# A layer norm folded into the dense layer behind attention, with smaller matmul bursts and a later weight preparation

## Chip, core and metric

The kernel runs on one core of a Trainium2 chip. The metric is the device time of one execution in microseconds (us), lower is better. TensorE is called PE here, ScalarE ACT, VectorE DVE, GpSimd POOL, and SyncE SP; SP issues all DMAs.

## What is computed

A pre-norm transformer block on x of 2 x 2048 x 1024 floats: latent attention with 32 heads whose keys have 4 numbers, and a dense layer with eight low-rank (LoRA) updates.

```python
x = x + attn(layernorm(x), ...)            # 32 heads, softmax over 2048 keys
# dense layer on layernorm(x):
h = jnp.einsum('bsd,nrd->nbsr', x, lora_A)
coef = (SCALE * lora_weights)[:, None, None]
lora_out = jnp.einsum('nbsr,nor->bso', h, lora_B * coef)
base = jnp.einsum('bsd,od->bso', x, W) + bias
# _layernorm: (x - mean) / sqrt(var + 1e-5), no gain, no bias
```

## The kernel before

The 4096 rows are taken in 8 chunks of 512 rows; a chunk is 4 tiles (t = 0 to 3) of 128 rows. A first stage (up to about 130 us) normalises x, computes the latents and stores query parts in DRAM. Then comes attention, chunk by chunk, in 128 steps each: step = 16 g + kt, g one of 8 groups of 4 heads, kt one of 16 key tiles. A step is: PE computes scores for 4 heads (L772), ACT takes two exponentials of 128 x 1024 (L562) out of PSUM, PE multiplies the results with the values (L783). PE's order is written out by hand in `attention`. In even steps PE does the scores and then the values of the two steps before; in odd steps it does the scores and then one piece of other work. Scores of a step wait for the first exponential of the step before (L770), values for their exponentials. PE is in order: a piece of work that waits holds scores and values behind it.

In chunk 0 the pieces are the preparation of weights (`prepare`): values (L701), LoRA (L707), the folded output weight (L719), biases (L726), and the dense weight `w_eff` in 16 blocks k: `turn_w(k)` transposes W (L737), `lora_update(k)` two steps later adds the LoRA product (L742), and DVE's `move_w(k)` (L1183 to L1189) takes both out of PSUM and splits the sum in a high and a low part. W lies in the stages `w_stage = [y, xn]`; SP's first load of a tile of x into y waits until the first half of W was read (L396), and the query loads `load_q` are queued behind it on SP. `W_BEFORE` blocks are prepared ahead of step 67, where the attention output of four groups is turned, the others after it.

In chunks 1 to 7 the pieces are the projection and the dense layer of the chunk before (`dense_beside`), all through the one PSUM bank SHARED. For each tile t: `project` (3 products into each of two halves, steps 7 and 9 for t = 0); DVE adds it to y and measures mean and variance (`residual`, `deviations`, 14 small operations in a chain); `normalise` writes xn (L995); from step TILE_AT[t] on PE turns xn in two pieces (`turn_xn`, L813) and DVE splits it into two parts (`move_xn`, L1017, L1019); then PE runs the dense layer in two halves of 24 products each (3 products for each of 8 blocks, L828), in bursts of at most `BURST` = 5 products: 5, 5, 5, 5, 4, one burst in each odd step; DVE adds the result to y (`add_dense`, L1239). POOL adds the attention bias to y when x has come, and the dense bias after xn was written (L470). Each tile has 28 steps: 4 for turning, 5 bursts, 2 projections of the next tile, 5 bursts.

After chunk 7's attention a tail does the same for the last chunk with nothing beside it: `project_last`, `turn_last` and `dense` on PE, on several banks.

Of the kernel before, what the change touches and what calls it, by code (L numbers as in the profile page):

```python
# [21 lines left out]
F32 = mybir.dt.float32  # L22
# [11 lines left out]
def build_block(nc, x, wq_d, bq_d, w_qk, b_qk, wkv_d, bkv_d, wv_u, bv_u, wo, bo,  # L34
# [38 lines left out]
    with ExitStack() as ctx:  # L73
# [76 lines left out]
        tight_f = sb("tight_f", [1, 1], F32)  # L150
        tight = sb("tight", [1, 1], I32)
        row_max = sb("row_max", [P, TT, H], F32)

        x_tiles = [y, xt_b]
        xn_tiles = [xn, xn_b]
# [24 lines left out]
        v_set, v_ln, v_lat, v_shift, v_rec, v_hi = (sem(n) for n in ("v_set", "v_ln", "v_lat", "v_shift", "v_rec", "v_hi"))  # L180
        prep_ps = sem("prep_ps")
        prep_ok = sem("prep_ok")
        x_in = [[sem(f"x_in{half}_{t}") for t in range(TT)] for half in range(2)]
        norm_ready = sem("norm_ready")
        xn_ready = sem("xn_ready")
# [86 lines left out]
        STORE_AT = [min(-(-(at + TILE_STEPS) // KT), G4 - 1) for at in TILE_AT]  # L272
# [162 lines left out]
        def _(pool):  # L435
# [137 lines left out]
        def _(pe):  # L573
# [155 lines left out]
            def turn_w(k):  # L729

                kb, half = k % KB, k // KB
                free_bank(PREP_W + 2 * k)
                pe.wait_ge(stage_in[half], 32)
                if k == W_BEFORE:
                    pe.wait_ge(o_normed, 1)
                for a in range(4):
                    last = nc.tensor.transpose(ps[:, SHARED, bass.ts(a, P)], w_stage[half][:, a, bass.ts(kb, P)], ident[:, :])  # L737
                last.then_inc(prep_ps, 1)
# [68 lines left out]
                                            start=(i == 0), stop=(i == 2))  # L807
                last.then_inc(proj_ready, 1)

            def turn_xn(p, t, u, bank):  # L810
                pe.wait_ge(xn_ready, (CHUNKS + p) * TT + t + 1)
                for a in range(4):
                    last = nc.tensor.transpose(ps[:, bank, bass.ts(a, P)], xn[:, t, bass.ts(4 * u + a, P)], ident[:, :])  # L813
                last.then_inc(t_ready, 1)

            def dense(p, t, half, kb, bank):
# [6 lines left out]
            PRODUCTS = [(kb, i) for kb in range(KB) for i in range(3)]  # L823

            def dense_burst(p, t, half, j):
                for kb, i in PRODUCTS[BURST * j:BURST * (j + 1)]:
# [3 lines left out]
                if j == BURSTS - 1:  # L830
                    last.then_inc(ffn_ready, 1)

            def dense_beside(c, step):

                p = c - 1
                if step == TURN_BACK_AT:
                    turn_back(p)
                if step == FIRST_AT:
                    pe.wait_ge(o_t_ready, p + 1)
                    project(p, 0, 0, SHARED)  # L840
                if step == FIRST_AT + 2:
                    pe.wait_ge(y_ready, START + p * TT * 2 + 1)
                    project(p, 0, 1, SHARED)
                if step == TURN_AT:
                    pe.wait_ge(ffn_moved, START + (p * TT + 2) * 2)
                    turn_o(c, 0)
                for t in range(TT):
                    at = step - TILE_AT[t]
                    if at == 0:
# [4 lines left out]
                        turn_xn(p, t, 0, SHARED)  # L854
                    if at == 2:
                        pe.wait_ge(t_moved, START + CHUNKS * KB + (p * TT + t) * 2 + 1)
                        turn_xn(p, t, 1, SHARED)
                    if t < TT - 1 and at == NEXT_AT:
                        pe.wait_ge(ffn_moved, START + (p * TT + t) * 2 + 1)
                        project(p, t + 1, 0, SHARED)  # L860
                    if t < TT - 1 and at == NEXT_AT + 2:
                        pe.wait_ge(y_ready, START + (p * TT + t + 1) * 2 + 1)
                        project(p, t + 1, 1, SHARED)
                    if at in DENSE_AT:
                        half, j = divmod(DENSE_AT.index(at), BURSTS)
                        if j == 0 and half == 0:
                            pe.wait_ge(t_moved, START + CHUNKS * KB + (p * TT + t + 1) * 2)
                        elif j == 0 and t < TT - 1:
                            pe.wait_ge(y_ready, START + (p * TT + t + 2) * 2)
                        elif j == 0:  # L870
                            pe.wait_ge(ffn_moved, START + (p * TT + t) * 2 + 1)
                        dense_burst(p, t, half, j)

            def attention(c, b, b_before=None):
                first = b_before is None
# [47 lines left out]
            def turn_last(t):  # L923
                for u in range(2):
                    if t:
                        pe.wait_ge(t_moved, START + CHUNKS * KB + (p * TT + t - 1) * 2 + u + 1)
                    turn_xn(p, t, u, 4 + u)

            project_last(0)
            project_last(1)  # L930
# [17 lines left out]
        def _(dve):  # L948
# [43 lines left out]
            def normalise(tiles=range(TT)):  # L992

                for t in tiles:
                    nc.vector.tensor_scalar(xn[:, t, :], y[:, t, :], mv[:, t, 0:1], nw[:, 0, 3, t:t + 1],  # L995
                                            ALU.subtract, ALU.mult).then_inc(xn_ready, 1)

            def split_shift(rows, bank, done, smallest=None, then=None):

# [160 lines left out]
            for half in range(2):  # L1160
                m = PREP_LORA + half
                dve.wait_ge(prep_ps, m)
                nc.vector.tensor_scalar(lora_bt[:, bass.ts(half, N)], ps[:, SHARED, :], coef, LORA_SCALE,
                                        ALU.mult, ALU.mult).then_inc(prep_ok, 1)
            for half in range(2):
# [82 lines left out]
            def tile_in(p, t):  # L1248
                ch = Chain(v_ln)
                residual(p, t, (SHARED, SHARED), ch)  # L1250
                deviations(ch, tiles=range(t, t + 1))
                normalise(range(t, t + 1))

            for c in range(1, CHUNKS):
                p = c - 1
# [1 line left out]
                norm_o(p, 1)  # L1257
                split_o(p)
                dve.wait_ge(t_ready, START + CHUNKS * KB + p * UNITS)
                tile_in(p, 0)  # L1260
                for t in range(TT):
                    move_xn(p, t, (SHARED, SHARED))
                    add_dense(p, t, 0)
                    if t < TT - 1:
                        tile_in(p, t + 1)
                    if t == 1:
                        move_o(c, 0)
                    add_dense(p, t, 1)
# [8 lines left out]
            for t in range(TT):  # L1277
                ch = Chain(v_ln)
                residual(p, t, (2 * (t % 2), 2 * (t % 2) + 1), ch)
                deviations(ch, tiles=range(t, t + 1))  # L1280
                normalise(range(t, t + 1))
                if t:
                    add_dense(p, t - 1, 0, 6)
                move_xn(p, t, (4, 5))
                if t:
                    add_dense(p, t - 1, 1, 7)
            for half in range(2):
# [26 lines left out]
```

## Time and profile before

| | |
|---|---|
| three runs | 2144.57, 2144.95, 2145.39 us (median 2144.95) |
| profiled execution | 2144.14 us, of which the span of its instructions 2142.2 us |
| busy | PE 1950.4 us (91%), ACT 2002.0 us (93%), DVE 508.9 us (24%), POOL 179.4 us (8%) |
| first exponential to last | 132.47 to 2070.48 us |
| tail after it | 71.7 us |
| chunk 0 of attention, chunk 3 | 244.85 us, 241.85 us |

The page gives busy times for each engine, the chain that ended last, and groups of instructions. Here it is best read together with the timeline: PE and ACT are both busy nine tenths of the span, and the timeline tells which of the two waits for the other in which steps.

### The profile page before, as it was taken

To read this page: it belongs to the slowest core of one execution; us is meant where nothing else is said; L and a number is where in the kernel's file an instruction comes from. 1 tells how busy PE (TensorE), PEld (TensorE's weight loads), DVE (VectorE), ACT (ScalarE), POOL (GpSimd) and SP (SyncE) were. 2 spreads that over 40 slices of the span, in tenths; PEclk is the share of its full clock that TensorE was granted. 3 is DMA by queue.
4 is the path that set the end of the run, shared out by engine and by line. 5 is a ranking of instruction groups with operands and counts; after the bars stand their busy time and mean duration, and the time that the engine had idled before them with its cause. 6 is when DMAs were issued, how large, how long until landed. Compare 5 with 4: busy or idle time off the path is not lost. (4 is left out here: it accounts for less than half of the span.)

```text
span 2142.2 us, 35926 instructions
## 1 busy us (share of the span) xinstructions
PE 1950.4 (91%) x15023; PEld 714.8 (33%) x15023; DVE 508.9 (24%) x1312; ACT 2002.0 (93%) x2193; POOL 179.4 (8%) x100
## 2 busy tenths in 40 slices
PE   4768898899989999899989999899999999899989
PEld 3412222233323333233323333333333333233337
DVE  8732231212111120212111120212112120212125
ACT  6969999999999999999999999999999999999960
POOL 1210001000110000100100000100100000100111
PEclk8979999999999999999999999999999999999999
DMA  7552000000010000100010000100010000100010
GB/s 240 180 142 69 30 25 23 5 15 25 15 43 5 25 25 13 35 15 25 13 44 5 25 17 20 35 15 25 13 44 5 25 14 24 35 15 25 13 40 40
DMA packets 45660, 77.41 MB, mean 36 GB/s; under 512 B 15870, under 2 KB 29750, under 8 KB 45498
## 3 DMA queue, kind: packets, MB, share of 16 engines
q1 hardware_dynamic: 45498, 75.11, 10.6%
q8 instruction: 119, 1.95, 0.4%
q14 instruction: 43, 0.35, 0.1%
HBM read 51.23 MB, written 23.86 MB: 35 GB/s over the span
## 5 line engine op out<-in xcount | busy, mean ns | idle before, releaser
L562 ACT ACTIVATE probs<-ps 128x1024 f32<-128x1024 f32 x2048 | 1908.5, 1029 | 41.8 <-PE ps L772 20.5
L783 PE MATMUL ps<-probs,c_wide 128*32 128x512 f32 x8192 | 989.5, 601 | 0.0
L772 PE MATMUL ps<-q_in,key_t 27*128 27x512 bf16 x4096 | 405.1, 386 | 131.7 <-ACT probs L562 124.0
L828 PE MATMUL ps<-w_eff,xn_t 128*128 128x512 f32 x1344 | 387.0, 416 | 0.0
L783 PEld LDWEIGHTS ps<-probs,c_wide 128*32 128x32 f32 x8192 | 213.2, 109 | 426.6 <-issue 235.3
L772 PEld LDWEIGHTS ps<-q_in,key_t 27*128 27x128 bf16 x4096 | 102.9, 91 | 752.4 <-ACT probs L562 737.3
L1239 DVE TENSOR_TENSOR y<-ps,y 128x512 f32<-128x512 f32 x64 | 44.2, 691 | 964.2 <-PE ps L828 953.7
L828 PEld LDWEIGHTS ps<-w_eff,xn_t 128*128 128x128 f32 x1344 | 230.4, 188 | 98.5 <-issue 63.4
L470 POOL TENSOR_TENSOR y<-y,ffn_bias 128x1024 f32<-128x1024 f32 x32 | 76.2, 2380 | 1163.7 <-DVE xn L995 1163.7
L466 POOL TENSOR_TENSOR y<-y,attn_bias 128x1024 f32<-128x1024 f32 x32 | 75.9, 2377 | 685.6 <-DMA y<-in_L_attn_x_dram 685.5
L1017 DVE CAST xn_t<-ps 128x512 fp32r<-128x512 f32 x64 | 44.2, 691 | 158.9 <-PE ps L813 158.9
L1223 DVE TENSOR_TENSOR y<-ps,y 128x512 f32<-128x512 f32 x64 | 44.2, 690 | 138.6 <-PE ps L806 138.6
L806 PE MATMUL ps<-w_vo,o_t 128*128 128x512 f32 x192 | 62.8, 442 | 1.8 <-DVE o_t L1019 1.8
L1019 DVE TENSOR_TENSOR xn_t<-ps,xn_t 128x512 fp32r<-128x512 f32 x64 | 44.3, 692 | 11.2 <-DVEq L968 11.2
L818 PE MATMUL ps<-w_eff,xn_t 128*128 128x512 f32 x192 | 45.9, 396 | 0.0
L813 PE MATMUL ps<-ident,xn 128*128 128x128 f32 x256 | 41.8, 289 | 3.6 <-DVE xn L995 3.6
L1226 DVE BATCH_NORM_STATS2 stats<-y 128x6 f32<-128x512 f32 x64 | 44.5, 695 | 2.2
L488 ACT ACTIVATE area<-ps 128x512 f32<-128x512 f32 x64 | 38.7, 627 | 5.8 <-PE ps L587 5.7
L806 PEld LDWEIGHTS ps<-w_vo,o_t 128*128 128x128 f32 x192 | 33.5, 198 | 18.5 <-issue 14.7
L818 PEld LDWEIGHTS ps<-w_eff,xn_t 128*128 128x128 f32 x192 | 36.0, 190 | 8.7 <-DVE xn_t L1019 1.3
L813 PEld LDWEIGHTS ps<-ident,xn 128*128 128x128 f32 x256 | 27.8, 143 | 17.1 <-issue 12.7
L482 ACT ACTIVATE xn<-y,nw 128x1024 f32<-128x1024 f32 x16 | 20.1, 1275 | 12.3 <-DVE nw L1028 12.3
(130 smaller groups left out, 591.0 us busy)
## 6 DMA issues: line engine op xcount, KB each, us to landing
y<-in_L_attn_x_dram SPq DMA_DIRECT2D x48, 512.0 KB, 4.2
out_dram<-y SPq DMA_DIRECT2D x32, 512.0 KB, 2.7
area<-in_L_attn_x_dram SPq DMA_DIRECT2D x16, 512.0 KB, 4.8
q_in<-q_parts SPq DMA_DIRECT2D x256, 27.0 KB
q_parts<-q_parts_sb SPq DMA_DIRECT2D x48, 128.0 KB, 2.1
y<-in_L_attn_Wo_dram SPq DMA_DIRECT2D x1, 2048.0 KB, 9.0
xn<-in_L_attn_Wo_dram SPq DMA_DIRECT2D x1, 2048.0 KB, 14.0
y<-in_L_ffn_W_dram SPq DMA_DIRECT2D x1, 2048.0 KB, 8.3
```

The source lines that it names most:

```text
L466: pool.tensor_tensor(y[:, t, :], y[:, t, :], attn_bias[:, :], ALU.add).then_inc(xb_ready, 1)
L470: pool.tensor_tensor(y[:, t, :], y[:, t, :], ffn_bias[:, :], ALU.add).then_inc(yb_ready, 1)
L562: nc.scalar.activation(probs[:, (c * STEPS + step) % PROBS, bass.ts(pair, 2 * N)], ps[:, 2 * (i % SCORE_SLOTS):2 * (i % SCORE_SLOTS) + 2, ...
L772: last = nc.tensor.matmul(ps[:, at, :], key_t[TILE * h:TILE * h + KEYS, bass.ts(b * KT + kt, P)], q_in[TILE * h:TILE * h + KEYS, g % 2, :] ...
L783: last = nc.tensor.matmul(ps[32 * h:32 * h + 32, SUMS, :], c_wide[:, b * KT + kt, at:at + 32], probs[:, (c * STEPS + step) % PROBS, bass.t ...
L806: last = nc.tensor.matmul(ps[:, bank, :], o_t[:, a, bass.ts(t, P)], w_vo[:, b, bass.ts(n, N)], start=(i == 0), stop=(i == 2))
L813: last = nc.tensor.transpose(ps[:, bank, bass.ts(a, P)], xn[:, t, bass.ts(4 * u + a, P)], ident[:, :])
L818: last = nc.tensor.matmul(ps[:, bank, :], xn_t[:, t % 2, a, kb, :], w_eff[:, b, kb, bass.ts(half, N)], start=(kb + i == 0), stop=(kb == KB ...
L828: last = nc.tensor.matmul(ps[:, SHARED, :], xn_t[:, t % 2, a, kb, :], w_eff[:, b, kb, bass.ts(half, N)], start=(kb + i == 0), stop=(kb == ...
L1017: ch.then(nc.vector.tensor_copy(high, bank_part))
L1019: nc.vector.tensor_tensor(low, bank_part, high.bitcast(F32), ALU.subtract).then_inc(moved, 1)
L1226: ch.put(nc.vector.bn_stats(stats[:, t, n, :], y[:, t, bass.ts(n, N)]))
```

## The change

The dense layer takes the raw tile instead of the normalised one. The mean is taken out of the weights: each row of W and of LoRA A is centred over its 1024 inputs (a sum, a small product and an addition on DVE, 9 times in all, in chunk 0), so that the product with a raw row equals that with the centred row. The row's 1/sqrt(variance) is multiplied in by `add_dense`, which becomes a scalar_tensor_tensor. `normalise` is gone from this part; `deviations` runs after `move_xn` as `finish`. PE's turning of a tile (`turn_y`) waits for y (both halves of the residual) instead of xn. POOL's dense bias waits in addition until the tile was turned. Each tile's first half has bursts of 4 products (6 bursts), the second half 5 as before (5, 5, 5, 5, 4). The positions become: TILE_AT 11, 41, 73, 103 (was 15, 43, 73, 101); bursts of the first halves from 15, 45, 77, 107; of the second from 31, 61, 93, 119; the last burst is in step 127 as before. In chunk 0 the values are turned in step 21 (was 17), `W_AT` is 53 (was 43), and `W_BEFORE` becomes 2 (was 5), so that the last `lora_update` is in step 123 (was 111).

```diff
-        DENSE_AT = (4, 6, 8, 10, 12, 18, 20, 22, 24, 26)
-        BURSTS = len(DENSE_AT) // 2
-        BURST = -(-3 * KB // BURSTS)
-        NEXT_AT = 14
-        TILE_STEPS = DENSE_AT[-1] + 2
+        BURST = ((4, 5), (4, 5), (4, 5), (4, 5))
+        BURSTS = [[-(-3 * KB // size) for size in sizes] for sizes in BURST]
...
-        TILE_AT = [15, 15 + TILE_STEPS, 17 + 2 * TILE_STEPS, 17 + 3 * TILE_STEPS]
-        TURN_AT = TILE_AT[2] - 2
+        at = FIRST_AT + 4
+        for t in range(TT):
+            if t == 2:
+                TURN_AT = at
+                at += 2
+            TILE_AT.append(at)
+            high = [at + 4 + 2 * j for j in range(BURSTS[t][0])]
+            NEXT_AT.append(high[-1] + 2)
+            low = [high[-1] + 2 + (4 if t < TT - 1 else 0) + 2 * j for j in range(BURSTS[t][1])]
+            DENSE_AT.append((high, low))
+            at = low[-1] + 2
...
-        VALUES_AT = 17
+        VALUES_AT = 21
...
-        W_AT = BIAS_AT + 4
+        W_AT = BIAS_AT + 10
...
                     pool.wait_ge(xn_ready, (CHUNKS + c) * TT + t + 1)
+                    pool.wait_ge(t_ready, START + CHUNKS * KB + (c * TT + t) * 2 + 2)
...
-                pe.wait_ge(stage_in[half], 32)
+                pe.wait_ge(w_centred, half + 1)
...
-            def turn_xn(p, t, u, bank):
-                pe.wait_ge(xn_ready, (CHUNKS + p) * TT + t + 1)
+            def turn_y(p, t, u, bank):
+                pe.wait_ge(y_ready, START + (p * TT + t + 1) * 2)
...
+            def centre(ch, rows, at):
+                total = row_sum[:, at:at + 1]
+                ch.then(nc.vector.tensor_reduce(total, rows, AX.X, ALU.add))
+                ch.then(nc.vector.tensor_scalar(total, total, -1.0 / D, None, ALU.mult))
+                ch.then(nc.vector.tensor_scalar(rows, rows, total, None, ALU.add))
...
+            ch = Chain(v_set)
+            centre(ch, lora_a_sb[:, :], KB)
+            ch.end()
...
-                nc.vector.tensor_tensor(y[:, t, bass.ts(half, N)], ps[:, bank, :], y[:, t, bass.ts(half, N)], ALU.add
-                                        ).then_inc(ffn_moved, 1)
+                nc.vector.scalar_tensor_tensor(out=y[:, t, bass.ts(half, N)], in0=ps[:, bank, :], scalar=nw[:, 0, 3, t:t + 1],
+                                               in1=y[:, t, bass.ts(half, N)], op0=ALU.mult, op1=ALU.add
+                                               ).then_inc(ffn_moved, 1)
...
+            for a in range(4):
+                centre_w(0, a)
             for k in range(W_BEFORE):
                 move_w(k)
             move_o(0, 0, True)
             norm_o(0, 0)
             for k in range(W_BEFORE, 2 * KB):
                 move_w(k)
+                if k < W_BEFORE + 4:
+                    centre_w(1, k - W_BEFORE)
...
+            def finish(ch, t):
                 deviations(ch, tiles=range(t, t + 1))
-                normalise(range(t, t + 1))
+                dve.sem_inc(xn_ready, 1)
...
-                tile_in(p, 0)
+                ch = tile_in(p, 0)
                 for t in range(TT):
                     move_xn(p, t, (SHARED, SHARED))
+                    finish(ch, t)
                     add_dense(p, t, 0)
```

## Rows read from the trace of the kernel before

**Rows 1.** The page, section 1: busy us (share of the span) and instructions of each engine

```profile
PE 1950.4 (91%) x15023; PEld 714.8 (33%) x15023; DVE 508.9 (24%) x1312; ACT 2002.0 (93%) x2193; POOL 179.4 (8%) x100
```

**Rows 2.** Windows: us, busy of PE, PEld, DVE, ACT, POOL, then clock, DMA share, GB/s

```profile
861.10:1102.95 241.85, 228.68 (x1800) 80.84 (x1796) 44.45 (x111) 238.81 (x257) 18.97 (x8) 1.00 0.07 22
...
132.47:377.32 244.85, 207.54 (x1709) 54.93 (x1713) 55.01 (x116) 236.64 (x256) 9.47 (x4) 0.97 0.18 54
```

**Rows 3.** Timeline of PE, chunk 3, steps 19 to 21: start, us, what, idle before

```profile
895.76 0.39 PE L772 MATMUL ps<-q_in,key_t 27*128 27x512 bf16 x4
896.08 1.43 PE L828 MATMUL ps<-w_eff,xn_t 128*128 128x512 f32 x5
897.44 0.39 PE L772 MATMUL ps<-q_in,key_t 27*128 27x512 bf16 x4
897.76 1.92 PE L783 MATMUL ps<-probs,c_wide 128*32 128x512 f32 x16
899.62 0.39 PE L772 MATMUL ps<-q_in,key_t 27*128 27x512 bf16 x4
```

**Rows 4.** Timeline of PE, chunk 3, steps 27 to 29, a burst of four

```profile
911.23 0.40 PE L772 MATMUL ps<-q_in,key_t 27*128 27x512 bf16 x4
911.55 1.19 PE L828 MATMUL ps<-w_eff,xn_t 128*128 128x512 f32 x4
912.74 0.40 PE L772 MATMUL ps<-q_in,key_t 27*128 27x512 bf16 x4
...
914.92 0.39 PE L772 MATMUL ps<-q_in,key_t 27*128 27x512 bf16 x4
```

**Rows 5.** Timeline of chunk 3: DVE's addition of step 9's projection, PE's scores of step 12

```profile
878.63 0.69 DVE L1223 TENSOR_TENSOR y<-ps,y 128x512 f32<-128x512 f32 x1 [2.18 <-PE ps L806]
...
882.51 0.40 PE L772 MATMUL ps<-q_in,key_t 27*128 27x512 bf16 x4 [1.12 <-ACT probs L562]
```

**Rows 6.** Two neighbours within a burst of five, and all dense products beside attention (min/median/max ns)

```profile
896.42 0.63 PE L828 MATMUL ps<-w_eff,xn_t 128*128 128x512 f32 x2
...
L828 PE MATMUL ps<-w_eff,xn_t x1344: 387/397/501, 412.4 to 2069.2; 128*128 128x512 f32 x192
```

**Rows 7.** Timeline of the tail, from the projections to the first dense product

```profile
2076.83 4.50 PE L806 MATMUL ps<-w_vo,o_t 128*128 128x512 f32 x12 [1.81 <-DVE o_t L1019]
...
2079.92 0.67 DVE L1223 TENSOR_TENSOR y<-ps,y 128x512 f32<-128x512 f32 x1
...
2084.92 1.97 PE L813 MATMUL ps<-ident,xn 128*128 128x128 f32 x8 [3.58 <-DVE xn L995]
...
2086.14 0.69 DVE L1017 CAST xn_t<-ps 128x512 fp32r<-128x512 f32 x1 [1.27 <-PE ps L813]
...
2089.24 1.43 PE L818 MATMUL ps<-w_eff,xn_t 128*128 128x512 f32 x3
```

**Rows 8.** Windows of the tail, columns as in rows 2

```profile
2086.90:2090.30 3.40, 3.40 (x9) 2.33 (x9) 3.09 (x5) 0.00 (x0) 0.40 (x1) 0.50 0.00 0
```

**Rows 9.** Timeline of ACT in chunk 0, steps 20 and 21

```profile
176.39 1.94 ACT L562 ACTIVATE probs<-ps 128x1024 f32<-128x1024 f32 x2 [3.03 <-PE ps L772]
...
179.83 1.94 ACT L562 ACTIVATE probs<-ps 128x1024 f32<-128x1024 f32 x2 [1.50 <-PE ps L772]
```

**Rows 10.** Groups of DVE by line and shape: busy us, mean ns, idle before

```profile
L995 DVE TENSOR_SCALAR xn<-y,mv,nw 128x1024 f32<-128x1024 f32 x32 | 26.0, 813 | 5.7 <-DVEq L968 5.7
...
L1040 DVE TENSOR_REDUCE c_max<-lat 128x1 f32<-128x512 f32 x8 | 5.4, 679 | 0.0
```

**Rows 11.** Timeline of chunk 0: SP after step 79, scores of step 91; last, the page's DMA issues

```profile
287.99 0.36 SPq L399 DMA_DIRECT2D y<-in_L_attn_x_dram  x1
...
288.39 1.43 SPq L342 DMA_DIRECT2D q_in<-q_parts  x4
...
308.65 0.40 PE L772 MATMUL ps<-q_in,key_t 27*128 27x512 bf16 x4
...
y<-in_L_attn_x_dram SPq DMA_DIRECT2D x48, 512.0 KB, 4.2
```

More of the change, by code:

```diff
@@ L259, in build_block @@
         SUMS, SHARED = 6, 7
[L263 to L267 removed]
+        BURST = ((4, 5), (4, 5), (4, 5), (4, 5))
+        BURSTS = [[-(-3 * KB // size) for size in sizes] for sizes in BURST]
         TURN_BACK_AT = BEHIND + 3
         FIRST_AT = BEHIND + 5
[L270 to L272 removed]
+        TILE_AT, NEXT_AT, DENSE_AT = [], [], []
+        at = FIRST_AT + 4
[9 more added lines that the diff above has]
+            at = low[-1] + 2
+        TILE_END = [low[-1] + 2 for high, low in DENSE_AT]
+        STORE_AT = [min(-(-at // KT), G4 - 1) for at in TILE_END]
         LOAD_AT = [min(g + 1, G4 - 1) for g in STORE_AT]
@@ L808, in project @@
                 last.then_inc(proj_ready, 1)
-            def turn_xn(p, t, u, bank):
-                pe.wait_ge(xn_ready, (CHUNKS + p) * TT + t + 1)
+            def turn_y(p, t, u, bank):
+                pe.wait_ge(y_ready, START + (p * TT + t + 1) * 2)
                 for a in range(4):
-                    last = nc.tensor.transpose(ps[:, bank, bass.ts(a, P)], xn[:, t, bass.ts(4 * u + a, P)], ident[:, :])
+                    last = nc.tensor.transpose(ps[:, bank, bass.ts(a, P)], y[:, t, bass.ts(4 * u + a, P)], ident[:, :])
                 last.then_inc(t_ready, 1)
@@ L825, in dense_burst @@
             def dense_burst(p, t, half, j):
-                for kb, i in PRODUCTS[BURST * j:BURST * (j + 1)]:
+                size = BURST[t][half]
+                for kb, i in PRODUCTS[size * j:size * (j + 1)]:
                     a, b = THREE[i]
@@ L829, in dense_burst @@
                                             start=(kb + i == 0), stop=(kb == KB - 1 and i == 2))
-                if j == BURSTS - 1:
+                if j == BURSTS[t][half] - 1:
                     last.then_inc(ffn_ready, 1)
@@ L847, in dense_beside @@
                 for t in range(TT):
-                    at = step - TILE_AT[t]
-                    if at == 0:
+                    if step == TILE_AT[t]:
                         if t == 2:
@@ L853, in dense_beside @@
                             pe.wait_ge(ffn_moved, START + (p * TT + t) * 2)
-                        turn_xn(p, t, 0, SHARED)
-                    if at == 2:
+                        turn_y(p, t, 0, SHARED)
+                    if step == TILE_AT[t] + 2:
                         pe.wait_ge(t_moved, START + CHUNKS * KB + (p * TT + t) * 2 + 1)
-                        turn_xn(p, t, 1, SHARED)
-                    if t < TT - 1 and at == NEXT_AT:
+                        turn_y(p, t, 1, SHARED)
+                    if t < TT - 1 and step == NEXT_AT[t]:
                         pe.wait_ge(ffn_moved, START + (p * TT + t) * 2 + 1)
                         project(p, t + 1, 0, SHARED)
-                    if t < TT - 1 and at == NEXT_AT + 2:
+                    if t < TT - 1 and step == NEXT_AT[t] + 2:
                         pe.wait_ge(y_ready, START + (p * TT + t + 1) * 2 + 1)
                         project(p, t + 1, 1, SHARED)
[L864 to L872, printed above, removed]
+                    for half in range(2):
+                        if step in DENSE_AT[t][half]:
+                            j = DENSE_AT[t][half].index(step)
+                            if j == 0 and half == 0:
+                                pe.wait_ge(t_moved, START + CHUNKS * KB + (p * TT + t + 1) * 2)
+                            elif j == 0 and t < TT - 1:
+                                pe.wait_ge(y_ready, START + (p * TT + t + 2) * 2)
+                            elif j == 0:
+                                pe.wait_ge(ffn_moved, START + (p * TT + t) * 2 + 1)
+                            dense_burst(p, t, half, j)
             def attention(c, b, b_before=None):
@@ L990, in deviations, with centre_w @@
                 ch.end()
[L992 to L996, printed above, removed]
+            def centre(ch, rows, at):
[3 more added lines that the diff above has]
+                ch.then(nc.vector.tensor_scalar(rows, rows, total, None, ALU.add))
+            def centre_w(half, a):
+                dve.wait_ge(stage_in[half], 32)
+                ch = Chain(v_set)
+                centre(ch, w_stage[half][:, a, :], half * 4 + a)
+                ch.end()
+                if a == 3:
+                    dve.sem_inc(w_centred, 1)
             def split_shift(rows, bank, done, smallest=None, then=None):
@@ L1164, in _ @@
                                         ALU.mult, ALU.mult).then_inc(prep_ok, 1)
+            ch = Chain(v_set)
+            centre(ch, lora_a_sb[:, :], KB)
+            ch.end()
             for half in range(2):
@@ L1284, in _ @@
                 move_xn(p, t, (4, 5))
+                finish(ch, t)
                 if t:
```

9 lines of the change are left out of this document (5 added, 4 removed).

## The prediction

> **What bounds the kernel now.** I read the page first: PE is busy 91% of the span and ACT 93% [rows 1], so the page alone doesn't say which of them sets the pace. Windows by chunk come next. Seven chunks of attention, 1 to 7, take 241.85 us each within 0.15 us, all at full granted clock [rows 2]; with chunk 0 they are 1938 of the 2142.2 us. Whatever one chunk gives counts seven times.
>
> The timeline of PE then shows two kinds of pairs of steps. Steps go in pairs, since the values are done for two at a time. In a pair with a burst of five products PE runs without a gap: scores 0.32 us (895.76 to 896.08), burst 1.36, scores 0.32, values 1.86, and the next pair's scores start at 899.62, 3.86 us after those of the first [rows 3]; the pair after it takes 3.87. Here PE is the bound and ACT waits. In a pair with a burst of four the scores follow at 911.23 and 914.92, 3.69 apart [rows 4], and pairs with three products or with four transposes have the same 3.69. In a step without other work PE stands idle for 1.12 us until an exponential is done [rows 5]. So 3.69 us is the pitch that the loop through ACT sets (scores, exponential, scores, values), whatever PE does beside it up to about four products; 3.865 is PE's own sum with five.
>
> The check: 64 pairs of 3.69 are 236.2 us. A chunk has 32 bursts of five (8 halves with four each) and takes 241.85. The remainder, 5.7 us, divided by 32 is 0.177 per burst, and the pitches differ by 0.175. The bursts of five explain all that a steady chunk takes beyond the loop.
>
> **Part by part.** *Bursts of four.* The first halves lose all their fives: 24 products in 6 bursts of 4. One more product in a burst costs about 0.23 us: two neighbours together last 0.63 us [rows 6], of which the second alone has 0.397, so starts are 0.23 apart. PE's own sum with four is thus 3.86 - 0.23 = 3.63 us, 0.06 under the loop's 3.69, and a run of fours piles up no delay, as each is below the pitch. The row of a four agrees: its burst and the gap behind it take 1.19 us (911.55 to 912.74) where the products need 1.36 - 0.23 = 1.13 [rows 3, 4]. Removed are 16 stalls of 0.175 us a chunk, 2.8 us; over seven chunks 19.6 us. The second halves keep theirs, 16 a chunk. For a stall the ends are 0.16 and 0.19, that is 18 to 21 us.
>
> A page of the Trainium skill gives another price. "TensorE: Matmul & The Clock Gate", section "Back-to-back issue gap", puts 512 columns at 512/2.4 plus 2.5 ns, 216 ns. By that rule five products would need 1.08 us instead of 1.36, a pair 3.59, and the fives wouldn't stall at all; the steady gain would be nil. The trace disagrees, with 3.86 measured and no gap in it [rows 3].
>
> *Room for them.* The four steps of a chunk that the extra bursts need come from turning tile 0 at step 11 instead of 15, and from the low half of tile 3, which now follows without a gap of four steps. The new wait is for both halves of y. In chunk 3 the projection of step 9 was added to y from 878.63 on in 0.69 us, by 879.32, and PE was through with the scores of step 11 and idle from 882.51 - 1.12 = 881.39 [rows 5], 2.1 us later. It doesn't wait. If it did, scores and values of the step stand behind it. In step 119 PE waits for the addition of tile 3's first half, which follows the burst of step 117 by some 0.8 us; a pair is 3.69 long.
>
> *Less on DVE.* `normalise` took 0.81 us a tile [rows 10], and the 14 small operations move behind the split. DVE is idle most of the time beside attention (44 us busy of 242 [rows 2]), so this is worth nothing there. POOL's bias addition (18.97 us for 8 of them, 2.4 each [rows 2]) starts after `finish`, about step 16, and is needed by the addition that follows the first half, at step 25 or later: covered by six bursts, 20 us. The scaled addition reads the same two operands of 512 as now (0.69); I price it the same, between -0.1 and +0.15 us, and it lies on the path once, at the very end.
>
> *Tail.* PE finishes the fourth projection at 2081.2 (the last of 12 products ends at 2081.33), y of tile 0 is done at 2080.6, and yet PE turns the tile only at 2084.92, after 3.58 us of idling for xn [rows 7]. This wait goes: PE turns at 2081.2, which is 3.7 us earlier. What is late next is DVE's split, which begins 1.22 us after the turning and ends 3.1 us after that (2086.14 to 2089.24). At full clock the 1.22 us shrink to an estimated 0.7, and the first dense product starts at 2081.2 + 0.7 + 3.1 = 2085.0, 4.2 us earlier than 2089.24. From there to 2138 PE is the only bound: 192 products, 32 transposes, 3 products of a projection twice. DVE's new order (finish before the addition of the tile before) puts up to 2.7 us on the second additions; the dense half that needs the bank starts over 4 us after the add was free to run, so I cost it at nothing, up to 0.5 us if tight.
>
> The clock bears on this. After the idle stretch PE's granted clock is 0.50, that is 1.2 GHz, up to 2090.3 while it is busy all of the time [rows 8]. Without the idle stretch the level may stay at 2.4 GHz, and then the first 1.1 us of dense work, done at half rate now, take 0.5 us less: 4.7 in all. If the clock falls anyway, only the 3.7 remain, and half rate over a stretch as that of rows 8 at a place where PE is the bound costs 1.7 once more. I take 4.5, between 2 and 5. The same page of the Trainium skill ("Why this matters for your kernels") advises against idle gaps between bursts since the clock drops after them; the trace agrees here, and by that advice the tail gives the whole 4.7.
>
> *Chunk 0.* It takes 244.85 us [rows 2], 8.7 more than 64 pairs. ACT waits 3.03 and 1.50 us where PE first waits for DVE's many small copies of the values and then runs slowly [rows 9]. With the values turned four steps later the copies, the distance of two steps and so the wait are the same: no change, from -1.5 (the clock stays up) to +1.7. Centring is new on DVE. A reduction over 512 is 0.68 us, so over 1024 about 1.2; the addition over 1024 is 0.81 as in L995 [rows 10] (with two scalar operands); with the small product and the waits in between an estimated 2.3 us. Four of them (9 us) lie between the bias of step 45 and `turn_w(0)` in step 53, 14.8 us later: covered, with some 3 us to spare after the bias has been moved. PE's new wait stands there; behind it are scores and values. The next four go between blocks that are four steps (7.4 us) apart, and there DVE has only a copy of 0.7 us to do in the 3.69 us between the transposes and the LoRA product: covered. The centring of A sits between the LoRA steps and the product of step 29: covered. W needs four further steps of y, so SP stands at the load of x until step 91 instead of 79, with the loads of queries for step 96 behind it. They were issued within 1.83 us after the release at 287.99 [rows 11], 1.5 us after the scores of step 79. So now: 308.65 + 1.5 + 1.8 = 312.0, plus a landing of 4.2 at most (that of a whole tile of x, 512 KB against 27 [rows 11]), 316.2; PE looks for them behind the scores of step 95, at 308.65 + 2 x 3.69 + 0.32 = 316.35. It just fits, and it happens once. Cost 0 to 3 us.
>
> **Sum.** Steady 19.6, tail 4.5, chunk 0 nothing: 24.1 us. The profiled execution took 2144.14 us with a span of 2142.2, so the span becomes 2118.1 and that execution 2120.0. The median of the runs is 0.8 above the profiled one: 2144.95 - 24.1 = 2120.9.
>
> **Rivals.** (a) Fours stall as well. Now a four always stands alone, followed by a pair with fewer products; in a run of six a delay could show that a single one hides. If each costs half of a five's 0.175, that is 24 x 0.09 x 7 = 15 us, and the time is 2136. If a four costs the whole 0.175, a chunk has 40 stalled pairs instead of 32, 9.8 us more in seven chunks, minus the tail's 4.5: 2150.3, slower than before. It turns slower from (32 x 0.175 + 4.5/7 - 16 x 0.175)/24 = 0.143 us a four. Against it: 3.63 is less than 3.69, and the gap behind the four in rows 4.
> (b) The preparation binds. Query loads late in step 95, or centring late for step 53: 3 to 9 us, 2124 to 2130. For it: a margin of 0.15 us by the upper price of the landing. Against it: a load of 27 KB should land well before one of 512 KB.
> (c) Fives fit under the loop too, and the 5.7 us of a chunk have a cause that stays: only the tail gives, 2144.95 - 4.5 = 2140.5. For it nothing in the rows; 3.86 us without a gap [rows 3] speak against it. The rule on the issue gap would lead to this rival.
> (d) The change doesn't do what it says: the earlier turn or another wait takes back in each chunk what the fours give (2.8 us), and the time stays within 4 us of now.
> (e) The clock stays up in the tail and in chunk 0: 2.0 us more than the sum, and up to 5 with lucky stretches: 2114 to 2118.
>
> **Chances.** Forecast (2117 to 2124) 0.70, (e) 0.06, (b) 0.09, (a) in part 0.07, (c) 0.01, (d) 0.03, (a) in full 0.04. The range 2116.5 to 2127.5 takes in the forecast and most of (b) and (e). About 0.2% (4.3 us) is what a measurement can tell from no change: faster 0.93, same 0.03, slower 0.04.
>
> **What would show it.** Chunks 1 to 7 of 239.0 us instead of 241.85; pairs with fours at 3.69 and with fives at 3.865, 16 of the latter a chunk; PE's wait in the tail gone and its first dense product about 4 us after the first turning; two waits of ACT in steps 24 and 25 of chunk 0 and none at steps 53 and 95. The prediction is wrong if pairs with fours take over 3.75, if PE waits at step 11, or if chunk 0 grows by more than 3 us.

## The result and the profile after

The changed kernel takes 2121.07 us (median of 4 runs, 2119.41 to 2122.61) against 2144.86 (4 runs) before. The ratio is 0.9889, with a 95% interval of 0.9872 to 0.9906. It is 23.8 us faster, where 24.1 were forecast.

| us | before | after | change | forecast |
|---|---|---|---|---|
| start to first exponential | 132.47 | 131.74 | -0.7 | 0 |
| chunk 0 | 244.85 | 248.19 | +3.3 | 0 |
| chunks 1 to 7, together | 1693.2 | 1673.9 | -19.3 | -19.6 |
| tail after the last exponential | 71.7 | 67.0 | -4.7 | -4.5 |
| span of the profiled execution | 2142.2 | 2120.8 | -21.4 | -24.1 |

The profiled execution of after (2122.6 us) is one of its slower ones; the median lies 1.5 us lower. The parts that were forecast as changed came out within 0.3 us each. Chunk 0, which was forecast as unchanged, did not: it grew by 3.3 us. The prediction names a growth of more than 3 us as a sign of being wrong, so by its own sign it is wrong in this part. Together with the earlier start, chunk 0 ends 2.6 us later than in before.

First the page, section 1, as in rows 1:

```profile
PE 1958.8 (92%) x15023; PEld 710.0 (33%) x15023; DVE 504.6 (24%) x1307; ACT 1993.5 (94%) x2193; POOL 180.0 (8%) x100
```

Then windows of chunk 3, chunk 0 and the tail; the columns are those of rows 2:

```profile
858.17:1097.24 239.07, 230.37 (x1800) 80.48 (x1796) 41.33 (x107) 237.58 (x257) 18.96 (x8) 1.00 0.07 22
131.74:379.93 248.19, 208.20 (x1709) 55.22 (x1713) 74.03 (x143) 236.77 (x257) 9.47 (x4) 0.97 0.18 54
2053.78:2120.80 67.02, 57.75 (x268) 45.68 (x264) 38.40 (x101) 0.00 (x1) 14.32 (x6) 0.97 0.15 55
```

Against rows 2, chunk 3 has the same 1800 matmuls in 2.78 us less, and DVE has 3.1 us less to do. In chunk 0 DVE is busy 74.0 us instead of 55.0, with 27 more instructions: those are the nine centrings of three operations each.

The timeline of PE in chunk 3, steps 23 to 25 (fours) and 31 to 33 (fives), answers rows 3 and 4. Columns are start, us, what, idle before:

```profile
900.22 0.39 PE L783 MATMUL ps<-q_in,key_t 27*128 27x512 bf16 x4
900.54 1.20 PE L840 MATMUL ps<-w_eff,xn_t 128*128 128x512 f32 x4
901.73 0.40 PE L783 MATMUL ps<-q_in,key_t 27*128 27x512 bf16 x4
902.06 1.92 PE L794 MATMUL ps<-probs,c_wide 128*32 128x512 f32 x16
903.91 0.39 PE L783 MATMUL ps<-q_in,key_t 27*128 27x512 bf16 x4
...
914.99 0.39 PE L783 MATMUL ps<-q_in,key_t 27*128 27x512 bf16 x4
915.32 1.42 PE L840 MATMUL ps<-w_eff,xn_t 128*128 128x512 f32 x5
916.67 0.39 PE L783 MATMUL ps<-q_in,key_t 27*128 27x512 bf16 x4
...
918.85 0.39 PE L783 MATMUL ps<-q_in,key_t 27*128 27x512 bf16 x4
```

A pair of steps with four products takes 3.69 us (900.22 to 903.91), one with five still 3.86 (914.99 to 918.85). The scores of step 11 start at 878.07 and those of step 31 at 914.99: ten pairs, six of them with fours, in 36.92 us. That is the pitch of 3.69 for all ten: a run of fours doesn't pile up a delay.

The timeline of the tail, against rows 7:

```profile
2060.14 4.53 PE L817 MATMUL ps<-w_vo,o_t 128*128 128x512 f32 x12 [1.81 <-DVE o_t L1040]
...
2064.51 1.04 PE L824 MATMUL ps<-ident,y 128*128 128x128 f32 x8
...
2065.22 0.69 DVE L1038 CAST xn_t<-ps 128x512 fp32r<-128x512 f32 x1 [0.58 <-PE ps L824]
...
2068.30 8.01 PE L829 MATMUL ps<-w_eff,xn_t 128*128 128x512 f32 x34 [1.36 <-DVE xn_t L1040]
```

The 3.58 us of idling before the turning are gone, and the split starts 0.71 us after it instead of 1.22. Counted from the last exponential, the first dense product starts after 14.5 us instead of 18.8. Two windows, with columns as in rows 8: the granted clock is still 0.50 while the first projections run, as it is in before, but full from the turning on, where rows 8 show 0.50:

```profile
2060.10:2063.40 3.30, 3.26 (x8) 2.61 (x9) 1.47 (x3) 0.00 (x0) 3.11 (x2) 0.50 0.01 4
2063.40:2066.80 3.40, 3.40 (x20) 2.65 (x18) 2.61 (x5) 0.00 (x0) 0.00 (x0) 1.00 0.00 0
```

Chunk 0 is the miss. The timeline of ACT and PE there, for rows 9:

```profile
161.17 1.36 SPq L352 DMA_DIRECT2D q_in<-q_parts  x4
...
164.96 0.39 PE L783 MATMUL ps<-q_in,key_t 27*128 27x512 bf16 x4 [3.86 <-DMA q_in<-q_parts]
...
165.39 1.94 ACT L573 ACTIVATE probs<-ps 128x1024 f32<-128x1024 f32 x2 [2.32 <-PE ps L783]
...
169.22 13.01 ACT L573 ACTIVATE probs<-ps 128x1024 f32<-128x1024 f32 x14 [1.89 <-PE ps L783]
...
185.62 1.94 ACT L573 ACTIVATE probs<-ps 128x1024 f32<-128x1024 f32 x2 [3.39 <-PE ps L783]
...
189.71 6.54 ACT L573 ACTIVATE probs<-ps 128x1024 f32<-128x1024 f32 x7 [2.15 <-PE ps L783]
```

The waits of rows 9 (3.03 and 1.50) are 3.39 and 2.15 now, four steps later, in steps 24 and 25. New is a wait of PE before step 16, for queries, followed by two waits of ACT.

### The profile page after: what moved, and what is told of

It is laid out like the page before. It is cut to its first block and busy times, and to the rows that moved or that the text cites. A ratio compares the mean times of both kernels' runs of the same rounds, so it can differ in the third digit from the quotient of the medians.

```text
span 2120.8 us, 35990 instructions
## 1 busy us (share of the span) xinstructions
PE 1958.8 (92%) x15023; PEld 710.0 (33%) x15023; DVE 504.6 (24%) x1307; ACT 1993.5 (94%) x2193; POOL 180.0 (8%) x100
## 5 line engine op out<-in xcount | busy, mean ns | idle before, releaser
L573 ACT ACTIVATE probs<-ps 128x1024 f32<-128x1024 f32 x2048 | 1900.1, 1030 | 34.3 <-PE ps L783 23.8
L840 PE MATMUL ps<-w_eff,xn_t 128*128 128x512 f32 x1344 | 394.6, 418 | 0.0
L1263 DVE SCALAR_TENSOR_TENSOR y<-ps,nw,y 128x512 f32<-128x512 f32 x64 | 48.0, 751 | 977.5 <-PE ps L840 967.7
L1247 DVE TENSOR_TENSOR y<-ps,y 128x512 f32<-128x512 f32 x64 | 44.2, 690 | 137.5 <-PE ps L817 137.1
L1040 DVE TENSOR_TENSOR xn_t<-ps,xn_t 128x512 fp32r<-128x512 f32 x64 | 44.3, 692 | 11.5 <-DVEq L980 11.5
L829 PE MATMUL ps<-w_eff,xn_t 128*128 128x512 f32 x192 | 45.4, 393 | 1.4 <-DVE xn_t L1040 1.4
L824 PE MATMUL ps<-ident,y 128*128 128x128 f32 x256 | 40.9, 285 | 0.0
L1221 DVE COPY o_sb<-ps 128x512 f32<-128x512 f32 x16 | 11.1, 692 | 86.6 <-PE ps L794 86.6
L824 PEld LDWEIGHTS ps<-ident,y 128*128 128x128 f32 x256 | 27.2, 140 | 13.2 <-issue 12.7
```

Source lines behind the costliest of these rows:

```text
L573: nc.scalar.activation(probs[:, (c * STEPS + step) % PROBS, bass.ts(pair, 2 * N)], ps[:, 2 * (i % SCORE_SLOTS):2 * (i % SCORE_SLOTS) + 2, ...
L824: last = nc.tensor.transpose(ps[:, bank, bass.ts(a, P)], y[:, t, bass.ts(4 * u + a, P)], ident[:, :])
L829: last = nc.tensor.matmul(ps[:, bank, :], xn_t[:, t % 2, a, kb, :], w_eff[:, b, kb, bass.ts(half, N)], start=(kb + i == 0), stop=(kb == KB ...
L1040: nc.vector.tensor_tensor(low, bank_part, high.bitcast(F32), ALU.subtract).then_inc(moved, 1)
L1263: nc.vector.scalar_tensor_tensor(out=y[:, t, bass.ts(half, N)], in0=ps[:, bank, :], scalar=nw[:, 0, 3, t:t + 1], in1=y[:, t, bass.ts(half, ...
```

## The experiments

### One part alone, and more of it

**Fives again.** The changed kernel with one line changed:

```diff
-        BURST = ((4, 5), (4, 5), (4, 5), (4, 5))
+        BURST = ((5, 5), (5, 5), (5, 5), (5, 5))
```

> The changed kernel with bursts of five in both halves; the fold, the earlier turning and the later preparation stay. Theory: PE's own sum with five products (3.865 us a pair) is what a chunk takes beyond the loop of 3.69, so the 16 stalls removed in each of seven chunks come back. Chunks 1 to 7 take 241.9 us instead of 239.1, the tail stays as in the changed kernel, and the time is the changed kernel's 2121.1 + 7 x 2.8 = 2140.8 (2139 to 2143). Rival: the gain came from the fold and its shorter waits; then the time stays within 3 us of 2121.

Measured: 2140.79 us (ratio to before 0.998, 0.9971 to 0.999), chunk 3 at 241.93 us. The tail stays short, 67.6 us. Its window of chunk 3:

```profile
861.50:1103.43 241.93, 228.68 (x1800) 80.87 (x1796) 41.30 (x106) 238.88 (x257) 18.92 (x8) 1.00 0.07 22
```

This is 19.7 us above the changed kernel: 19.7 of the 23.8 us need the fours. The fold by itself, with less work on DVE and the shorter wait, gives nothing in a steady chunk (241.93 against 241.85).

**Sixes.** The same with more in each burst; tile 0 starts at step 15, so that the output of the fourth group is ready:

```diff
-        BURST = ((4, 5), (4, 5), (4, 5), (4, 5))
+        BURST = ((6, 5), (6, 5), (6, 5), (6, 5))
...
-        at = FIRST_AT + 4
+        at = FIRST_AT + 8
```

> The changed kernel with four bursts of six products in the first halves (tile 0 turned in step 15), five in the second ones. Theory: PE is the bound in each pair above four products and one product costs 0.235 us, so a pair with six takes 4.10 us, 0.41 above the loop's 3.69: 16 of them a chunk, 6.6 us, 45.9 us in seven chunks; chunks of 245.7 us and a time of 2121 + 46 = 2167 (2163 to 2171). Rival: a stall costs the same whatever the burst's length above four (a missed slot, not a sum); then the chunks take 241.9 and the time is 2141.

Measured: 2167.69 us (1.0106, 1.0086 to 1.0126), chunk 3 at 245.60 us. The pitch with six is in its timeline of PE, steps 21 to 23:

```profile
909.41 0.40 PE L783 MATMUL ps<-q_in,key_t 27*128 27x512 bf16 x4
909.74 1.66 PE L840 MATMUL ps<-w_eff,xn_t 128*128 128x512 f32 x6
911.33 0.40 PE L783 MATMUL ps<-q_in,key_t 27*128 27x512 bf16 x4
...
913.51 0.39 PE L783 MATMUL ps<-q_in,key_t 27*128 27x512 bf16 x4
```

It is 4.10 us: PE's sum grows by 0.235 us a product. With four, five and six products a pair takes 3.69, 3.865 and 4.10; the line has its bend just above four. The rival of a fixed price falls.

**Fours without the fold.** The kernel before, its schedule written with the changed kernel's loop, from step 15, with fours in tiles 0 and 1 only:

```diff
-        DENSE_AT = (4, 6, 8, 10, 12, 18, 20, 22, 24, 26)
...
+        BURST = ((4, 5), (4, 5), (5, 5), (5, 5))
...
+        at = FIRST_AT + 8
```

> The kernel before with nothing of the fold: bursts of four in the first halves of tiles 0 and 1 (as many as the steps allow there), five elsewhere. Theory: 8 stalls of 0.175 us fewer in each of seven chunks, 24 instead of 32, so chunks 1 to 7 take 240.45 us, the tail stays 71.7 us and the time is 2144.9 - 9.8 = 2135.1 (2134 to 2137). Rival: fours do good only together with the fold; then the chunks stay at 241.85 and the time at 2144.9.

Measured: 2142.72 us (0.9992, 0.9982 to 1.0002, which can't be told from no change), chunk 3 at 241.70 instead of 240.45. The expectation missed by 7.6 us. Chunk 3 has 24 stalls of a five, as expected, and one new wait in step 66. Its timeline:

```profile
977.45 0.69 DVE L1232 TENSOR_TENSOR y<-ps,y 128x512 f32<-128x512 f32 x1 [2.19 <-PE ps L814]
...
981.59 0.81 DVE L1004 TENSOR_SCALAR xn<-y,mv,nw 128x1024 f32<-128x1024 f32 x1 [0.18 <-DVEq L977]
...
982.32 0.69 DVE L1206 COPY o_sb<-ps 128x512 f32<-128x512 f32 x1
...
983.06 1.92 PE L791 MATMUL ps<-probs,c_wide 128*32 128x512 f32 x16 [1.18 <-DVE o_sb L1206]
```

The extra burst of tile 1 moves the projection of tile 2 to step 63. From there DVE runs the additions, the chain of small operations and the normalisation, and only then copies the attention sums of the first four groups out of PSUM, which PE's values of step 66 need. PE waits 1.18 us each chunk, 1.25 us of the chunk's time; seven of them are 8.8 of the 9.8 us.

**The same fours elsewhere**, to tell whether that stall was all. Against the last kernel:

```diff
-        BURST = ((4, 5), (4, 5), (5, 5), (5, 5))
+        BURST = ((5, 5), (5, 5), (4, 5), (4, 5))
```

> The kernel before without the fold, bursts of four in the first halves of tiles 2 and 3 instead of 0 and 1, so that the projection of tile 2 stays in step 59. Theory: the 8 fives left out give 8 x 0.175 us a chunk; e2_fours lost them to one stall of 1.25 us in step 66, where DVE still ran the chain of the norm and the normalisation ahead of its copy of the attention sums. Here that copy is in time: chunks of 240.45 us, no long wait of ACT in step 66, a time of 2144.5 - 9.8 = 2134.7 (2133 to 2137). Rival: fours need the fold everywhere; the chunks then stay near 241.7 and the time at 2142 to 2144.

Measured: 2136.12 us (0.9955, 0.9938 to 0.9971) beside 2145.5 for before, a gain of 9.4. Chunk 3 takes 240.47 us:

```profile
860.00:1100.47 240.47, 229.53 (x1800) 80.65 (x1796) 44.49 (x111) 238.20 (x257) 18.98 (x8) 1.00 0.07 22
```

This is inside the expected range. Fours work without the fold, at the price per stall that was forecast, where they move nothing that DVE has to do in time.

### The tail

PE turns tile 0 only when the chain of small operations is through:

```diff
             def turn_last(t):
+                if t == 0:
+                    pe.wait_ge(xn_ready, (CHUNKS + p) * TT + 1)
                 for u in range(2):
```

and DVE runs `finish` of tile 0 ahead of `move_xn`.

> The changed kernel, where in the tail PE turns tile 0 only after DVE's chain of small operations for it (as the kernel before did, but without the 0.8 us of normalisation); nothing else changes. Theory: the wait that the change removed comes back less 0.8 us, 2.9 us, and with it a stretch of low clock: the tail takes 70.0 to 71.2 us instead of 67.0 and the time is 2124.5 (2123.5 to 2125.5). Rival: DVE's split and the clock absorb the earlier turning, the tail's gain came from the shorter work on DVE alone; then the tail stays under 68 us.

Measured: 2124.13 us, 3.1 above the changed kernel's 2121.07; the tail takes 71.3 us, against 67.0. PE idles 2.82 us, and the window behind it shows the clock (columns as in rows 2):

```profile
2065.49 1.97 PE L824 MATMUL ps<-ident,y 128*128 128x128 f32 x8 [2.82 <-DVEq L1286]
...
2065.40:2068.80 3.40, 3.31 (x12) 3.02 (x13) 1.90 (x3) 0.00 (x0) 1.25 (x1) 0.50 0.00 0
```

The eight transposes take 1.97 us as in rows 7, not 1.04: behind the idling the granted clock is 0.50. The wait and the clock make the tail's gain, and the rival (less work on DVE) falls. The tail is 0.1 us longer than forecast for it.

### The preparation

The changed kernel with early positions. Four blocks stand ahead of step 67:

```diff
-        VALUES_AT = 21
+        VALUES_AT = 17
...
-        W_AT = BIAS_AT + 10
+        W_AT = BIAS_AT + 4
...
-        W_BEFORE = (4 * KT - W_AT) // 4
+        W_BEFORE = 4
```

> The changed kernel with the early positions of the preparation: values in step 17, the first block of W in step 43, right behind the bias of step 41, with four blocks ahead of step 67. Theory: the later preparation is what hides the centring. DVE centres four rows of tiles (4 x 2.37 us) from the end of the bias on, PE waits about 7.4 us for them in step 43 with scores and values behind it, ACT some 6.3, and the clock falls once more for 1 to 2 us: a time of 2121 + 7.5 = 2128.5 (2126.5 to 2130). Rival: the centring is short enough to hide at the old place, and later preparation does nothing: within 2 us of 2121.

Measured: 2132.6 us (0.9946, 0.9929 to 0.9962), 11.5 above the changed kernel and 2.6 above the expected range. The timeline at step 43:

```profile
227.18 0.75 DVE L1009 TENSOR_SCALAR y<-y,row_sum 128x1024 f32<-128x1024 f32 x1
...
228.26 1.09 PE L748 MATMUL ps<-ident,y 128*128 128x128 f32 x4 [7.64 <-DVEq L1017]
...
229.93 1.94 ACT L573 ACTIVATE probs<-ps 128x1024 f32<-128x1024 f32 x2 [7.34 <-PE ps L783]
...
233.90 4.71 ACT L573 ACTIVATE probs<-ps 128x1024 f32<-128x1024 f32 x5 [2.03 <-PE ps L783]
```

The mechanism is as expected, PE idles 7.64 us for DVE's centring (7.4 were expected), but ACT loses 7.3 and 2.0, 9.4 us, where 7.5 were taken. A further 1.2 us come from step 85, where the block that opens the second half of W follows right behind the last centring: steps 85 and 86 start 3.03 us apart instead of 1.85, with a wait of ACT of 1.09 us. That is this variant's own. The rest of the miss, about 1 us, is not traced to one cause: with the values at their early place ACT waits 11.1 us in steps 16 to 21, against 9.8 in steps 16 to 25 of the changed kernel. The later place of the preparation is thus needed: it hides four centrings, 9 us of DVE work that the fold added.

### The queries of step 16

In chunk 0 SP issues the load of LoRA B and of Wo (4 MB) ahead of the queries for steps 16 to 31. In the next kernel the queries go first (`load_q(0, 1, 1, q_loaded[1])` ahead of them, and nothing at g = 0 of chunk 0):

> The changed kernel, with SP issuing the queries of step 16 ahead of the loads of LoRA B and Wo (4 MB) instead of behind them. Theory: PE's wait of 3.9 us behind step 15 and the fall of the clock after it (ACT waits 2.3 and 1.9 us) go, and chunk 0 no longer grows when attention starts early: first exponential plus chunk 0 give 375.5 to 376.5 us instead of 379.9, and the time is 2121 - 4 = 2117 (2115 to 2118.5). Rival: the queries land late for another reason (their own 108 rows of 1 KB); then nothing moves.

Measured: 2116.11 us (0.986, 0.9844 to 0.9877). The wait of PE before step 16 is gone, and the exponentials run from 138.83 to 177.76 without a gap; chunk 0 ends at 374.5 us instead of 379.9 (375.5 to 376.5 were expected). The gain is 5.0 us, 1.0 more than the most likely value and within the range. The timeline of ACT:

```profile
138.83 38.93 ACT L576 ACTIVATE probs<-ps 128x1024 f32<-128x1024 f32 x42 [2.07 <-PE ps L786]
180.59 1.94 ACT L576 ACTIVATE probs<-ps 128x1024 f32<-128x1024 f32 x2 [2.82 <-PE ps L786]
184.29 216.26 ACT L576 ACTIVATE probs<-ps 128x1024 f32<-128x1024 f32 x234 [1.77 <-PE ps L786]
```

The same edit in the kernel before:

> The kernel before, with the queries of step 16 issued ahead of LoRA B and Wo. Theory: the late queries are no part of the change. In the profiled execution of before, attention began at 132.5 us and they came just in time; where it begins earlier, PE waits. So before gains as well: first exponential plus chunk 0 fall from 377.3 to 373 to 375, the time from 2145 to 2142 (2140.5 to 2143.5). Rival: only the changed kernel pays for the late queries; then before stays within 1 us of 2145 and the step that was missed belongs to the change.

Measured: 2140.27 us (0.9979, 0.9969 to 0.9988), a gain of 4.5, 0.2 us more than the range had. The late queries belong to both kernels. The profile of before caught an execution in which attention began late (132.47), so that hardly a wait for the queries shows in it. The two kernels above that have before's chunk 0 and only other bursts behind it show the wait: 3.41 us in the one with fours in tiles 0 and 1, and in the one with late fours

```profile
164.09 0.54 PE L780 MATMUL ps<-q_in,key_t 27*128 27x512 bf16 x4 [4.06 <-DMA q_in<-q_parts]
```

Their chunk 0 takes 248.4 and 248.0 us, as that of the changed kernel does (248.2). It is the 244.85 of rows 2 that is the exception.

A second profile of the changed kernel:

> The changed kernel once more, for a second profile of it. Its four times came in two groups, 2119.5 and 2122.6 us. Theory: the 3.1 us lie in chunk 0, where PE's wait for the queries of step 16 and its wait in step 23 let the clock fall or not; chunks 1 to 7 and the tail take 239.1 and 67.0 us in either group. If this profile falls in the faster group, chunk 0 takes some 245 us instead of 248.2, with one stretch of low clock fewer in it. Rival: the difference lies in the tail's clock; then the tail takes 64 or 70 us.

Measured: 2120.12 us (2119.44 to 2122.69; ratio 0.9883). The profile fell among the slower times again, so the groups can't be told apart by it. The chunks are at 239.1 again and the tail at 67.0. Attention began 1.9 us earlier (129.85) and chunk 0 took 2.1 us longer (250.27). PE waited for the queries until 165.26, nearly the same moment as in the first profile (164.96), and in before they came by 165.1. Here all that attention gained by the early start was lost at the queries' landing. The wall isn't fixed, though: in the traces of the variants with the late queries PE gets them at 162.4 to 164.4, each time 12.8 to 13.4 us after SP began to issue them, and in two of them with the changed kernel's chunk 0, where attention began 4.4 us earlier than in the first profile (127.3), chunk 0 ended 1.8 and 2.3 us earlier.

### The values

The values turned in step 17 again, with LoRA B left in steps 23 and 25:

```diff
-                if step == VALUES_AT:
+                if step == VALUES_AT - 4:
```

> The changed kernel, with the values turned in step 17 as before, while LoRA B stays in steps 23 and 25. Theory: DVE's 32 small copies (7.3 us with what goes before) fit into six steps (11 us), so PE doesn't wait in step 23 and the clock doesn't fall: ACT's waits of 3.4 and 2.15 us in steps 23 and 24 go, 5.5 us, and the time is 2115.6 (2114 to 2117.5). Rival: the later place of the values was needed since LoRA B and the values weren't in SBUF by step 17; then PE waits in step 17 instead and the gain is under 2 us.

Measured: 2117.59 us (0.9867, 0.9851 to 0.9884), a gain of 3.5 instead of 5.5, 0.1 us outside the range. ACT's two waits behind the values (they stood in steps 24 and 25) are gone:

```profile
164.75 1.94 ACT L573 ACTIVATE probs<-ps 128x1024 f32<-128x1024 f32 x2 [1.83 <-PE ps L783]
168.05 3.77 ACT L573 ACTIVATE probs<-ps 128x1024 f32<-128x1024 f32 x4 [1.36 <-PE ps L783]
173.27 227.34 ACT L573 ACTIVATE probs<-ps 128x1024 f32<-128x1024 f32 x246 [1.45 <-PE ps L783]
```

but the low clock behind the queries' wait now lasts longer. These are the windows at that place, first of this kernel, then of the changed one:

```profile
168.90:172.30 3.40, 3.17 (x20) 0.70 (x20) 2.96 (x17) 2.92 (x4) 0.00 (x0) 0.50 0.00 0
...
169.00:172.40 3.40, 2.28 (x24) 0.51 (x20) 0.00 (x0) 3.18 (x4) 0.00 (x0) 1.00 0.02 5
```

PE takes 3.23 us instead of 1.92 for the values' products there, and ACT waits once more at 173.27 (1.45 us). The rival doesn't show: PE doesn't wait in step 17.

**Both together:**

> The changed kernel with both: queries of step 16 issued first, values turned in step 17. Theory: the two waits are independent and in series on PE, so the gains add: 4 + 5.5 us, a time of 2111.5 (2109.5 to 2113.5), chunk 0 at 239 to 241 us. Rival: the later of the two waits was partly caused by the first (the clock), so that together they give no more than 7 us: 2114 or above.

Measured: 2112.07 us (2108.82 to 2115.57; ratio 0.9849, 0.9833 to 0.9866), within the range, the fastest of all, and 9.0 below the changed kernel. After the first six exponentials and one wait of 2.07 us ACT never stops:

```profile
127.11 5.61 ACT L576 ACTIVATE probs<-ps 128x1024 f32<-128x1024 f32 x6 [8.77 <-PE ps L786]
134.78 266.14 ACT L576 ACTIVATE probs<-ps 128x1024 f32<-128x1024 f32 x288 [2.07 <-PE ps L786]
```

Chunk 0 takes 238.56 us, against 248.19. The profiled execution is the fastest of the four, 3.3 us below the median. The two gains add: 5.0 and 3.5 alone, 9.0 together. Its times spread more than others' (6.8 us). The likely reason is that an early or late start of attention is no longer evened out at the queries' landing; one trace can't show it. All three gains are counted from 2121.07; the second set of the changed kernel, 2120.12, would make each about 1 us smaller.

## Why the prediction was right, point by point

*What bounds the kernel.* Right, and shown: the loop of 3.69 us and PE's own sum cross between four and five products. The fours, fives and sixes give 3.69, 3.865 and 4.10, and chunks of 239.1, 241.9 and 245.6 us. Taking the number of such pairs times the difference of two pitches, and checking it against a whole chunk before using it, held to 0.3 us in 19.6. A steady chunk of after takes 239.07 to 239.11 us, and 239.05 by that sum. With this rivals (a) and (c) fall: six fours in a row keep the pitch of 3.69, and the fives bring the time of a chunk back to 241.9.

*Room in the schedule.* Right: `turn_y` in step 11 waits for nothing (878.07 plus five pairs of 3.69 is where step 21 starts, 896.53). The fours without the fold show what the forecast had passed over: the schedule has a second deadline, DVE's copy before step 66, and a late projection with the long chain behind it breaks it. In the changed kernel the projection of tile 2 stays in step 59, and the chain behind it was shortened, so this didn't matter; rival (d) would have been this.

*Price of a burst.* The products are 0.235 us apart in these bursts, and its ends cost 0.185 more (1.36 - 5 x 0.235 for five, by rows 3). With them fives don't fit. The 216 ns that the Trainium skill ("TensorE: Matmul & The Clock Gate", section "Back-to-back issue gap") gives for isolated products with 512 columns would have made the steady gain nil, and so would the 131 ns that the same section gives for a stream of weight loads and products. The measured 235 ns decides against both here.

*Tail.* Right, 4.7 against 4.5 taken. The turning is 3.7 us earlier and the first dense product 4.2, since the split follows it after 0.71 us, where 0.7 was estimated; the rest is the clock, as in the case where it stays up. Putting the wait back costs 3.1 us of median and 4.3 in the profiled tail. That the two profiles agree with the forecast to 0.2 us is partly luck: the tail takes 70.8 to 72.3 us in the four traces with before's tail and 66.7 to 68.0 in the eight with the changed one, 4.2 us apart on average, and it is longer where its mean granted clock is lower (0.97 at 67.0 us, 0.94 at 68.0).

*The scaled addition* was priced at nothing to 0.15 us. It takes 0.75 instead of 0.69 us (the last piece of the chain that ended last, 2116.93 in after), 0.06 on the path, once.

*Chunk 0.* The centring and SP's hold until step 91 cost nothing, as forecast: ACT has no wait at steps 53 and 95. The wrong part is that chunk 0 would stay, between -1.5 and +1.7 us. It grew by 3.3 us in the profiled execution, more than the 3 that the prediction allowed itself, and it ended 2.6 us later than in before. Of it 1.0 us is a longer low clock behind the values (3.39 + 2.15 against 3.03 + 1.50), and the rest is the queries' landing before step 16, which I didn't look at, since the trace of before shows only 0.1 us of waiting there. Most of this is no effect of the change. The same edit helps the kernel before by 4.5 us, and before's own chunk 0 takes 248.0 us, with waits of 3.39 and 2.17 behind the values, where attention begins at 130.99. A part may be: where attention begins at 127.3 to 127.6 us, chunk 0 takes 250.3 and 250.8 us with the values in step 21 and 248.4 with them in step 17 (fours in tiles 0 and 1), and these are single traces. The medians came out 0.2 us from the forecast although chunk 0 didn't behave as forecast. That closeness is luck: the changed kernel's four times spread over 3.2 us, and the second set was 24.4 us below its before instead of 23.8.

*The clock.* Behind the long idle stretches of PE (3.58 us in the tail of before, 2.82 with the wait put back, 3.86 before step 16, 3.66 behind the values) the granted clock was 0.50. In the tail the forecast took nearly the whole effect, in chunk 0 a range around nothing, and there the range was too narrow. The advice of the Trainium skill on idle gaps ("TensorE: Matmul & The Clock Gate", section "Why this matters for your kernels") agrees with the tail: the eight transposes take 1.97 us behind the gap and 1.04 without it. Of the 4.7 us it is the smaller part, as 3.7 are the wait itself.

## What to carry to other kernels

Where two engines are both above 90%, look for the pitch of one round of the loop in the timeline and write down how it depends on what is put beside it: here it is flat up to four products; the fifth adds 0.175 us, and the sixth its full 0.235. The fours cost nothing here beyond the loop's pitch, so it was worth spreading the same work over more rounds, even though that needed a rework of the dependencies to find the rounds. A transfer that comes just in time in one profile can take back a gain ahead of it; here it paid to issue the small load that a stage needs first before its large ones. And before a difference between two profiles is laid to a change, look at further traces of the same code: here a single profile of before showed the exception.

## What was not expected of the hardware

- In these bursts the f32r products with 512 columns start 0.235 us apart, with a new stationary operand for each; in the tail 36 of them take 8.16 us, 0.227 each. A burst of five between scores and scores takes 1.36 us.
- A scalar_tensor_tensor of 128 x 512 from PSUM took 751 ns, a tensor_tensor of the same operands 691 ns. A tensor_scalar of 128 x 1024 took 754 ns with one operation and 813 with two. A reduction over 1024 took 1.21 us.
- Times of one kernel that differ by 3 us without a disturbance were not noise of the steady part: the steady chunks of one kernel agreed to 0.15 us in all traces, while the start (first exponential at 127.1 to 132.5 us), chunk 0 and the tail (66.7 to 68.0 us with the same code) did not.
